# Where eight experts' weights are cut into high and low halves under attention: pieces evenly spaced and loaded earlier

## The reference

```python
x = x + attn(layernorm(x))      # 16 heads of 16, causal softmax, W_qkv, W_out
xn = layernorm(layernorm(x)) * gamma + beta     # the second one is the FFN's own
probs = softmax(xn @ gate_w)    # 8 experts, the best 2 of a token, shares made to sum to 1
h = gelu(xn @ w1[e] + b1[e])    # w1: 8 x 256 x 1024
out_e = h @ w2[e] + b2[e]       # w2: 8 x 1024 x 256
x = x + sum_e share[e] * out_e + layernorm(x)
```

## Time and profile before

| | us |
|---|---|
| median of 3 executions | 1029.56 (1025.6 to 1031.1) |
| the profiled execution, its own time | 1028.05 |
| its span in the trace | 1026.3 |
| PE busy | 885.7 (86%) |
| DVE busy | 721.0 (70%) |
| ACT busy | 583.8 (57%) |
| units 12 to 27, in which 26 pieces are cut | 236.55 |

### The profile page before, as it was taken

The page is one execution under the profiler, slowest core; times in us unless marked ns, Lnnn a source line. Parts: engine busy times, 40 slices in busy tenths (PEclk is TensorE's granted clock), DMA queues, the critical chain, the costliest instruction groups (busy, mean ns, idle before and its releaser), DMA issues.

```text
span 1026.3 us, 21292 instructions
## 1 busy us (share of the span) xinstructions
PE 885.7 (86%) x6870; PEld 569.9 (56%) x6870; DVE 721.0 (70%) x1658; ACT 583.8 (57%) x1078; POOL 465.1 (45%) x561
## 2 busy tenths in 40 slices
PE   4989858887787978878788798999989999999996
PEld 3654413232332424233242587778977998988875
DVE  6677848788578786887766386676666766766664
ACT  3766437666658686765757373554534545545453
POOL 2000013344434756565475746474565554544441
PEclk9999959796786878678686899899999999999998
DMA  9987767765656466563724642224223322233221
GB/s 216 285 256 268 230 190 221 214 157 175 212 157 195 130 176 184 166 199 96 205 71 123 230 94 56 48 34 100 44 43 49 58 49 46 46 58 48 38 48 19
DMA packets 149528, 134.29 MB, mean 131 GB/s; under 512 B 58448, under 2 KB 132048, under 8 KB 149296
## 3 DMA queue, kind: packets, MB, share of 16 engines
q1 hardware_dynamic: 118416, 90.13, 30.8%
q0 software_dynamic: 15680, 18.95, 11.4%
q10 hardware_dynamic: 15328, 23.86, 7.3%
HBM read 83.63 MB, written 48.99 MB: 129 GB/s over the span
## 4 chain that ended last, share of the span: by engine, by line
PE 53%; DMA 15%; DVE 12%; issue 7%; SPq 6%; ACT 4%; another core or an unknown queue 1%; ACTq 0%; POOL 0%; POOLq 0%; DVEq 0%
PE banks L754 17%; PE banks L771 16%; DMA arena<-in_L_ffn_w 6%; PE banks L573 3%; PE banks L676 3%; PE banks L632 3%; PE banks L688 2%; DMA weighed_values<-arena 2%; PE banks L563 2%; SPq L1852 2%; PE banks L617 2%; DVE arena L1211 2%; DVE arena L1213 1%; SPq L1867 1%
## 5 line engine op out<-in xcount | busy, mean ns | idle before, releaser
L975 ACT ACTIVATE arena<-banks,arena 128x256 f32<-128x256 f32 (+1 forms) x312 | 152.2, 541 | 194.1 <-issue 131.7
L754 PE MATMUL banks<-arena,weights 128*128 128x256 f16 (+1 forms) x1872 | 211.5, 268 | 17.9 <-issue 16.7
L754 PEld LDWEIGHTS banks<-arena,weights 128*128 x1872 | 175.1, 99 | 49.9 <-issue 24.9
L771 PE MATMUL banks<-weights,arena 128*128 x1704 | 196.6, 274 | 1.6 <-DVE arena L1495 1.2
L1685 POOL DMA_INDIRECT out<-arena x71 | 116.0, 1634 | 175.1 <-DVE arena L1506 139.2
L771 PEld LDWEIGHTS banks<-weights,arena 128*128 128x128 f16 x1704 | 165.9, 98 | 24.1 <-issue 3.7
L632 PE MATMUL banks<-arena 50*128 50x128 f16 (+3 forms) x512 | 128.5, 358 | 45.8 <-ACT arena L901 13.4
L604 PE MATMUL banks<-arena 48*128 48x384 f16 (+3 forms) x512 | 108.0, 352 | 33.9 <-DMA arena<-qk_parts 15.1
L1493 DVE TENSOR_SCALAR arena<-arena 128x512 f16<-128x512 f32 (+1 forms) x156 | 77.1, 495 | 79.1 <-ACT arena L975 73.0
L632 PEld LDWEIGHTS banks<-arena 50*128 50x128 f16 x512 | 38.4, 102 | 161.2 <-issue 57.8
L1495 DVE SCALAR_TENSOR_TENSOR arena<-arena 128x512 f16<-128x512 f32 (+1 forms) x156 | 110.1, 706 | 5.6
(11 more groups left out here) (188 smaller groups left out, 1304.5 us busy)
## 6 DMA issues: line engine op xcount, KB each, us to landing
weights<-in_L_ffn_w ACTq DMA_DIRECT2D x16, 1024.0 KB, 8.1
arena<-in_L_ffn_w SPq DMA_DIRECT2D x32, 512.0 KB
qk_parts<-weights SPq DMA_DIRECT2D x96, 128.0 KB
arena<-qk_parts SPq DMA_DIRECT2D x128, 96.0 KB, 3.8
weighed_values<-arena SPq DMA_DIRECT2D x32, 256.0 KB, 5.0
token_rows<-arena SPq DMA_DIRECT2D x12, 512.0 KB, 4.2
arena<-weighed_values SPq DMA_DIRECT2D x32, 128.0 KB
arena<-inverse_sums SPq DMA_DIRECT2D x32, 128.0 KB
```

What stands on the lines that cost most here:

```text
L754: m = pe.matmul(bank[:, c * TILE:c * TILE + WIDTH[j]], w1[:, k, wp, f:f + P], xp[:, k, 0:WIDTH[j]], start=(i == 0), stop=(i == len(terms) ...
L771: m = pe.matmul(bank[:, c * D:(c + 1) * D], hp[:, f, c * P:(c + 1) * P], w2[:, f // (FC // 2), wp, f % (FC // 2), :], start=(f == 0 and i ...
L975: m = act.activation(h_32[r % 2][:, c, 0:WIDTH[j]], banks[:, 1 + c2, c * TILE:c * TILE + WIDTH[j]], ACT.Gelu, bias=b1_now[j % 2][:, 2 * c2 ...
```

## The change

The times in ticks at which the pieces stand are replaced.

- The first six: one each 40 ticks from 410 on in place of one each 38, loaded 22 ticks ahead in place of 20.
- The other 26: before, at ticks 66, 84, 114, 130, 146, 162 and 178 of batches 3 to 6 (the last of them cut short after five), so that seven pieces stand 16 to 30 ticks apart and then none for 80. Now one each 26 ticks from 650 to 1300. They are loaded 35 ticks ahead in place of 20.

The first of the 26 was at tick 642 and is at 650; the last was at 1298 and is at 1300. Nothing else changes.

```diff
-        split_ticks = [410 + 38 * i for i in range(LENT)]
-        split_ticks += [base + tick for base in range(3 * NG * UNIT, 7 * NG * UNIT, NG * UNIT)
-                        for tick in (66, 84, 114, 130, 146, 162, 178)][:W_SPLITS - LENT]
+
+        split_ticks = [410 + 40 * i for i in range(LENT)]
+        split_ticks += [650 + 26 * i for i in range(W_SPLITS - LENT)]
         for i, base in enumerate(split_ticks):
-            at(base - 20, "load_raw", i)
+            at(base - (22 if i < LENT else 35), "load_raw", i)
             at(base, "high_weights", i)
             at(base + 9, "low_weights", i)
```

## The result

The change made the kernel faster by 1.4%: a median of 1012.96 us (4 executions, 1009.38 to 1022.63) against 1030.33 us for the kernel before in the same series, ratio 0.9858, 95% interval 0.9817 to 0.9898. The prediction had 1014 us from 1029.56 us. The profiled execution of the changed kernel has a span of 1009.8 us, 16.5 less than before.

What follows compares the result with a forecast made beforehand. Late weight-piece loads, 23.6% of the chain from 300 to 520 us, were taken to stall the whole core. Terms -3.7 - 1.9 - 9.0 + 0.9 - 2.0 = -15.7 us gave 1014 us, forecast 1005 to 1021, 8-in-10 range 998 to 1027.

Steps and rivals of the forecast that it cites:

- signs of being wrong: Units like 15 growing over 1 us each, SP's low-half waits beyond 14.3 us, or waits gone but long units at 16.
- kind D: Attention units held by PE, such as unit 15: five new pieces cost +0.9 us, between 0 and +5.7.
- 4.6 us covers each: Loads of the 26: 4.6 us more lead covers every wait but the first, the longest being 3.0 or 3.1 us.
- kind C: Long attention units 14, 18, 22 and 26: half of 17.9 us of waits comes back, -9.0 us.
- Kind A: Attention units near DVE's limit, such as 12 and 16: -3.7 us in unit 12, -1.9 us in the others.
- Kind B: Attention units such as 17, keeping two pieces each, no waits in unit 17: taken as unchanged.
- SP should stand less: SP's loads of the 26: 8 ticks behind the low half freeing their buffer, not 3, so SP waits less.
- rival 3: Slower: SP waits for low halves and `top_in` comes late for the next unit's scores; about 1045 us, chance 0.06.
- The first six: First six pieces: two ticks more lead shorten the four waits behind the first, 7.7 us in all, by -2.0 us.
- The seam: `load_raw(6)` moves ahead of the low half it waits for; SP stands 1.2 to 4.3 us, costed at nothing.
- That rule's rival: Little comes back: other chains fill gaps, new pieces pay up to 8 us on DVE; about 1028 us, chance 0.20.
- Rival 1: More comes back: all waits of the 26 are on the path, PE's granted clock rises; 992 to 1002, chance 0.17.

Runs made afterwards that it cites:

- Lead alone: Kernel before with its old places in bursts, the 26 pieces loaded 35 ticks ahead in place of 20, plus a third buffer: 1012.82 us, ratio 0.9869.
- spacing alone: Changed kernel with its new even places, but loads 20 ticks ahead as before: 1027.75 us, ratio 1.0017.
- the square: Kernel before and changed kernel, each with low halves whole or 8 columns, all on one expert's weights: 1000.04, 986.33 (whole), 998.49, 968.27 us (8 columns).
- The third buffer: Changed kernel with a third buffer for the loads of the 26 pieces: 1017.46 us, ratio 0.9885.

## Why the prediction was right

It said 1014 us by -15.7; the medians moved by 17.4 and the ratio by 14.6 us. The mechanism is right, loads that land late and lead that mends them. That the number is so close is in part luck. Units 12 to 27 were to give 13.7 us and gave 11.6 and 12.0, as more came back in C and was lost in B and D; in the first trace another 1.9 us in units 28 to 30 and the 2.7 us of scatter ahead of attention, neither of them forecast, brought the span to -16.5. Of its signs of being wrong one came true (SP's waits beyond 14.3 us) and another nearly (kind D by 1.0 us a unit in the first trace), and the waits of 13.3 and 12.3 us are over the 12 that it gave; the first was a poor sign, as shown below. Its steps:

- **Loads that land late stop the whole core, and lead mends it: shown.** Lead alone has the gain, spacing alone none. 35 ticks leave 3.0 and 1.7 us of waits. But a tick of lead does not take a tick off each wait, as the prediction's "4.6 us covers each" has it: 28 ticks are 2.5 us more than 20, spacing alone had eleven waits of 3.7 us at most, and 12.4 us stayed. Why is open.
- **"I take half" for kind C: mis-sized.** Kind C gave 11.7 and 13.1 us for 9.0, two thirds to three quarters of its 17.9. Of the 5 or 6 us that it kept, low halves hold 1.6 in the square. Whether PE's order and clock keep the rest, as the prediction had it, was not tested.
- **Kind A, -5.6, "since DVE is full": right.** It gave 8.3 and 5.0 us; unit 12 alone gave 4.5 and 2.3 (priced at 3.7). The reason is the one that the square shows: low halves that lay in the stalls are on the path once the stalls are gone, and without them kind A falls by another 10.2 us. Their share of the chain rose too.
- **"Kind B ... is taken as unchanged": failed.** It grew by 4.3 and 4.7 us, and by 5.2 with lead alone, where its pieces stayed in place. In unit 17 before, ACT was busy for all 11.03 us; now it is busy for 11.27 of 12.58. My reading is that ACT caught up there with what the stalls of kind A had left it. A stall is then partly made good a unit later, and that part never was to be had. The traces show the full unit before and the growth after. In the square kind B grows as much without low halves, so it isn't DVE's doing. I did not test the backlog by itself.
- **Kind D, +0.9: too low if anything**, +4.1 and +1.4 us, inside the bounds of 0 to 5.7. With lead alone and no pieces there it is +0.1, and in unit 19 the chain now passes a low half. But unit 27, which has no piece in either kernel, grew by 1.5 and 0.9 of these, so what the new pieces cost in D is not clear of the scatter. Kind C is shorter by 1.0 and 2.4 us than the 54.95 with lead alone. The times of the two kernels are the same, so moving pieces into the free-looking unit bought nothing measurable.
- **"SP should stand less": failed, and harmless.** It stood 27.5 and 26.3 us for 14.3. With the load 35 ticks ahead, it stands 8 ticks behind a low half that DVE does late; in the bursts only some loads did. The third buffer took this away for no gain, so rival 3's mechanism exists and has no price here that was measured.
- **The first six, -2.0: failed**, 0.2 to 0.45 us in units 8 to 11. The waits of the five behind the first did not fall from 7.7 us but rose, to 10.4 and 10.7. The first piece's own wait only changed its name, from 4.5 us for the load to 4.0 for the scales (L1200), as the prediction had it. The load of one buffer follows a low half by 9 ticks in both versions; that this is why two ticks more don't help is my reading.
- **The seam, at nothing:** SP stood 2.3 and 7.1 us for the last low half of the first six, where 4.3 was the most that I named. Unit 12 took 13.17 us in the first of these traces and 15.41 in the second; whether that is the price was not tested.
- **The stage of the experts at nothing: right**, 460.8 and 460.66 us from unit 30's copy.
- **Low halves beside POOL's additions.** The low half's mean over the 26 was 1.53 us before and 1.47 and 1.48 us in the two profiles after, so the new places pay no more to POOL, as costed, though one low half took 3.89 us at the start of unit 23. That rule's rival did not come about.
- **Rival 1's clock.** The granted clock over units 12 to 27 is 0.77 before and 0.80 in both traces after; what it is worth was not parted from the rest.

Unit by unit, the two traces of the changed kernel differ by up to 2.3 us, and their sums of four by up to 3.3, so a single unit or kind is weak evidence; the sums of all sixteen agree within 0.4.

## What to carry to other kernels

Ask of a stall on one engine what the others do inside it. Work that lies in a stall is free until the stall is mended, and then it is the next bound: here 28 us of waits were worth 14 us with DVE's work in place, and 35 us of them 30 without it. When a change moves both when a load is issued and where its consumer stands, the two can be parted with one more buffer, and here all that was measured was in the lead. A unit that looks unchanged by a stall ahead of it may still grow when the stall is mended, so such a unit is not safely priced at nothing.

## What the runs showed of the hardware that I had not expected

A low half cut to 8 columns should take as little as its shortest, 0.21 us. Beside POOL's addition over 128 x 1024 it took 2.75 us (the kernel at the places of before with low halves of 8 columns; L1704 is `with_bias` there):

```profile
400.07 2.75 DVE L1367 SCALAR_TENSOR_TENSOR weights<-arena,weights 128x8 f16<-128x8 f32 x1
400.43 2.35 POOL L1704 TENSOR_TENSOR arena<-arena 128x1024 f32<-128x1024 f32 x1
```

The whole low half met such an addition and took 2.91 us. The short one ended at 402.82 us, POOL's at 402.78. So what it pays is the rest of POOL's instruction and not a share of its own length. The Trainium skill describes such an exclusive lock, held for a whole instruction by whichever starts first (SBUF — State Buffer, section "SBUF: two separate sides"). The trace agrees that the one waits for the other to end; who started first it doesn't bear out, since DVE's record starts 0.36 us ahead of POOL's, and starts on POOL are rough in a profile.

Chips differ by 2% on this kernel: the kernel before took 1026, 1008 and 1005 us on three. In the profiles much of it lies in the stage of the experts: from unit 30's copy to the end 460 to 463 us in the four kernels on the first, 441.3 and 441.6 us in the two with all experts' weights on the second, with the granted clock at 0.97 and 0.99. Why is open.
